# Transfers cut to multiples of sixteen rows, keys stored alone, scales ahead of the branch, and the sorted path as the fall-through

## The chip, the cores and the metric

The kernel runs on one core of a Trainium2 chip. The core has five engines with instruction streams of their own: TensorE (PE, with its weight loads shown as PEld), VectorE (DVE), ScalarE (ACT), GpSimd (POOL) and SyncE (SP), which here only issues transfers. They meet through semaphores. The metric is the device time of one execution in microseconds; times of an unchanged kernel agree within about 0.2%.

## What is computed

A chain of four residual layers over 3125 nodes with 256 features and 50,000 edges, all in float32: a graph convolution, an attention over slices, a hypergraph convolution of two steps, and a mixture of experts. The change touches the first and, by a few rows, the last. Cut to what matters here:

```python
src, dst = edges sorted by dst                      # 50,000 pairs of node numbers

x = x + gnn(layernorm(x))                           # the section of this change
    src, dst = concat(src, 0..n-1), concat(dst, 0..n-1)
    deg  = segment_sum(1, dst)
    dinv = 1 / sqrt(deg)
    agg  = segment_sum((xn @ W)[src] * dinv[src] * dinv[dst], dst)
    return relu(agg + b)
x = x + slice_attention(layernorm(x))
x = x + hypergraph_convolution(layernorm(x))
x = x + experts(layernorm(x))                       # top 2 of 8, summed into out
```

## The kernel before

**Layout.** The nodes are padded to 3200, 25 chunks (c) of 128 rows; `XR` holds x in this layout (tile `residual`), `Z` the scaled or normed rows. The last chunk has only 53 rows (`LAST`). The graph becomes a dense matrix of edge counts, source by target, built in five blocks of 640 targets (`SB`), and the aggregation is a product with it. `XH2` keeps the rows as a high and a low float16 half, so that float16 products are exact enough.

**First block.** VectorE clears the id tiles, GpSimd makes constants, and SyncE loads `dst` and `src` as 125 rows (`ER`) of 400 numbers, and the first number of each next row as 124 single numbers (`nxt`). It waits for them, and the block ends for all engines.

**Front of the main block.** VectorE and ScalarE build `triple`, three words per edge (`front_dve`, `front_act`). SyncE (`front_sp`) stores it to `packed_dram`, the keys, behind the first two groups of five row chunks, and sends the other three groups and the last 53 rows right after it. VectorE finds the start position of each group of five targets (`place`, `w_pos`). GpSimd (`front_pool`) waits for the stores (`st`) and the positions, and gathers 128 keys per group of targets in five indirect transfers into `win`. TensorE turns them (`keys_turn_pe`), VectorE compares them with node numbers (`keys_dve`), TensorE counts degrees. In between VectorE and ScalarE take row sums and squares of x, whenever a group of rows is there (`row_statistics_dve`, `row_sums_act`, `row_squares_act`). At the end VectorE writes `flag`: 1 if the edges are not sorted or a group has more than 128 of them.

**Branch.** Each engine waits for `flag`, loads it into a register and takes `If`, the general path, or `Else`, the sorted path. For these inputs it is the sorted path. The general path stands first in each instruction stream, so that the sorted one is reached by a jump.

**Sorted path.** First `scales_dve` and `scales_act`: VectorE makes `lnscale` and `lnshift`, ScalarE scales the rows of five groups (`scaled_rows_act`), VectorE cuts them into high and low halves (`low_rows_dve`: five casts L602, five subtractions L605). A quad is four groups of five targets: VectorE makes two tiles of one-hots (`quad_dve`, L498 and L499), TensorE multiplies them (`quad_pe`, L508, one of four banks), ScalarE copies the counts out (`quad_act`, L519). There are 160 quads, 32 in each block, and 16 of them (`AHEAD`) are made before the main loop. The loop runs over five blocks b and 32 slots s: each slot makes quad 16 further on and an eighth of a quarter of the aggregation (`quarter_pe`, L1111). A quarter at s = 0 or s = 16 first waits until the copies of the quads that it reads are done. Six idle products (L355) stand between the leading quads and the loop. Then follow first products, relu, residual, statistics and the normed rows for the next section.

**Last section.** Before the experts, SyncE stores the rows to `out`, 3072 rows and then the 53 (L2153); GpSimd's first accumulating scatter waits for both (`xr_st`).

## Time and profile before

| | us |
|---|---|
| median of three runs (lowest, highest) | 1334.64 (1334.37, 1336.47) |
| the profiled execution, its own time | 1334.33 |
| its span, first to last instruction | 1332.6 |
| TensorE busy (matrix products) | 1242.6, 93% |
| VectorE busy | 570.0, 43% |
| ScalarE busy | 473.7, 36% |
| GpSimd busy | 198.2, 15% |
| mean granted TensorE clock | 0.969 of full speed |

The span divides into the front and the leading quads (0 to about 68 us), the main loop of the first layer (to 264), its end (to 276), the attention (to 403), the hypergraph convolution (to 1052), the routing (to 1098) and the experts. A busy share over the whole span says little about the front, where TensorE mostly waits. In rows of the order in time, the first number is the start in us, the second the length; square brackets give the idle time of the engine before it and what ended it. PEq, DVEq and SPq are the instruction queues of these engines.

### The profile page before, as it was taken

The page shows a single profiled execution, that of the slowest core. Times are in us where ns is not written, and L with a number is a line of the kernel's source. Part 1 is how long each engine was busy: PE and PEld are TensorE (multiplying, and loading weights), DVE is VectorE, ACT ScalarE, POOL GpSimd, SP SyncE. Part 2 cuts the span into 40 slices and gives each one's busy share as a digit, 9 for nine tenths or more (in the row PEclk, how much of TensorE's full clock was granted, in tenths as well). Part 3 has the DMA queues.
Part 4 walks back from the last instruction along what each step waited for, and adds up shares of the span by engine and source line. Part 5 has one row for each costly group of instructions (what it writes and reads, how often), then busy time and mean ns, then how long its engine had stood idle before and what let it go on. Part 6 is the DMA issues. An engine that isn't in the chain of part 4 may idle for free. (4 is left out here: it accounts for less than half of the span.)

```text
span 1332.6 us, 19869 instructions
## 1 busy us (share of the span) xinstructions
PE 1242.6 (93%) x7442; PEld 844.6 (63%) x7442; DVE 570.0 (43%) x1529; ACT 473.7 (36%) x1142; POOL 198.2 (15%) x201
## 2 busy tenths in 40 slices
PE   3399999989999999999999999999999878999995
PEld 1277777745558544457777544467777547888884
DVE  5878777567764413123333333222222471222221
ACT  5765666357743787830000010001222302222221
POOL 3000000023310000000000000000000005767773
PEclk8599999999999999999999999999999889999998
DMA  5132133400003155575556445587653264666662
GB/s 178 38 124 73 56 121 125 139 28 0 1 0 126 43 157 155 154 157 126 124 128 140 128 148 149 152 188 168 143 120 68 64 198 136 146 142 149 157 156 44
DMA packets 253597, 154.91 MB, mean 116 GB/s; under 512 B 172536, under 2 KB 242375, under 8 KB 253364
## 3 DMA queue, kind: packets, MB, share of 16 engines
q1 hardware_dynamic: 242420, 138.56, 38.0%
q0 software_dynamic: 11072, 14.97, 6.1%
q8 instruction: 64, 1.05, 0.3%
q14 instruction: 41, 0.34, 0.1%
HBM read 78.48 MB, written 35.00 MB: 85 GB/s over the span
## 5 line engine op out<-in xcount | busy, mean ns | idle before, releaser
L974 PE MATMUL bank<-weights,agg_in_out 128*128 128x320 f16 x2000 | 274.8, 299 | 0.0
L988 PE MATMUL bank<-weights 128*128 128x512 f16 x1250 | 270.7, 379 | 1.2 <-issue 1.2
L974 PEld LDWEIGHTS bank<-weights,agg_in_out 128*128 128x128 f16 x2000 | 195.7, 98 | 76.2
L988 PEld LDWEIGHTS bank<-weights 128*128 128x128 f16 x1250 | 122.0, 98 | 149.3 <-DVEq L1786 1.7
L1111 PE MATMUL bank<-weights,agg_in_out 128*128 128x320 f16 x1000 | 163.2, 299 | 0.0
L804 POOL TENSOR_TENSOR shift<-shift,rstd 128x5 f32<-128x5 f32 x15 | 3.6, 243 | 914.6 <-ACT rstd L809 914.6
L519 ACT CAST weights<-bank 128x500 f16<-128x500 f32 x160 | 114.2, 723 | 68.9 <-PE bank L508 68.9
L1111 PEld LDWEIGHTS bank<-weights,agg_in_out 128*128 128x128 f16 x1000 | 91.7, 98 | 26.2
L2258 PE MATMUL bank<-weights 128*128 x448 | 105.5, 384 | 0.5 <-ACT weights L2274 0.2
L2274 ACT ACTIVATE weights<-bank,weights 128x256 f32<-128x256 f32 (+1 forms) x128 | 50.2, 444 | 155.4 <-PE bank L2243 155.4
L2243 PE MATMUL bank<-wk,weights 128*128 128x256 f32 (+1 forms) x512 | 104.2, 357 | 0.9 <-DVE wk L2289 0.9
L1784 DVE SCALAR_TENSOR_TENSOR wk<-bank,inverse_degree,wk 128x256 f32<-128x256 f32 x50 | 24.0, 480 | 181.9 <-ACT wk L1980 181.9
L2336 POOL DMA_INDIRECT out<-weights,agg_in_out x56 | 89.3, 1595 | 61.4 <-DVE weights L2304 34.5
L2243 PEld LDWEIGHTS bank<-wk,weights 128*128 128x128 f32 x512 | 89.5, 193 | 12.0 <-issue 1.2
L2258 PEld LDWEIGHTS bank<-weights 128*128 128x128 f32 x448 | 80.7, 190 | 15.9 <-issue 7.2
L1019 ACT COPY agg_in_out<-bank 128x320 f32<-128x320 f32 x20 | 8.5, 426 | 218.5 <-PE bank L974 218.5
L508 PE MATMUL bank<-wn,wk 128*128 128x125 f16 x640 | 64.8, 227 | 18.2 <-DVE wn L499 17.6
L1027 DVE COPY agg_in_out<-bank 128x320 f32<-128x320 f32 x20 | 9.8, 491 | 161.1 <-PE bank L974 141.0
L498 DVE TENSOR_TENSOR wk<-iota,low_source 128x512 f16<-128x512 f16 x160 | 67.4, 421 | 25.9 <-PE bank L508 25.1
L1980 ACT ACTIVATE wk<-bank,inverse_degree 128x256 f32<-128x256 f32 x50 | 23.6, 474 | 153.2 <-PE bank L988 142.3
L508 PEld LDWEIGHTS bank<-wn,wk 128*128 128x128 f16 x640 | 49.6, 101 | 34.3 <-DVE wn L499 22.8
L2316 POOL DMA_INDIRECT normed<-rows_and_gates,agg_in_out x56 | 59.0, 1054 | 58.5 <-POOLq L1759 41.7
(355 smaller groups left out, 1455.8 us busy)
## 6 DMA issues: line engine op xcount, KB each, us to landing
weights<-counts_source_target SPq DMA_DIRECT2D x50, 800.0 KB, 4.6
counts_source_target<-weights SPq DMA_DIRECT2D x5, 4000.0 KB, 13.9
weights<-in_L_ffn_W SPq DMA_DIRECT2D x32, 512.0 KB, 3.9
weights<-in_L_ffn_W SPq DMA_DIRECT2D x4, 1024.0 KB, 5.5
rows_and_gates<-normed SPq DMA_DIRECT2D x1, 3300.0 KB, 12.0
out<-residual SPq DMA_DIRECT2D x1, 3072.0 KB
residual<-in_x SPq DMA_DIRECT2D x4, 640.0 KB, 7.9
weights<-in_L_ffn_b SPq DMA_DIRECT2D x1, 1024.0 KB, 7.6
```

The lines of the kernel that those rows point to most:

```text
L498: nc.vector.tensor_tensor(couples(ohs[:, u]), ramp(4, P), twins(slo2[:, g, :], P), ALU.is_equal)
L508: last = nc.tensor.matmul(ps[QBANK[u]][:, t * NR:(t + 1) * NR], ohs[:, u, t, :], ohr[:, u, t, 0:NR], start=True, stop=True)
L519: nc.scalar.copy(to, ps[QBANK[q % 4]][:, 0:4 * NR].rearrange("p (t n c) -> p t c n", t=4, c=NC)).then_inc(q_ev.sem, 1)
L974: last = nc.tensor.matmul(bank, source[:, 5 * k + c, part * F + fh * P:part * F + fh * P + P], MB[:, k, c, h * HALF:(h + 1) * HALF], start ...
L988: last = nc.tensor.matmul(ps[j][:, :], MB[:, k, c, j * P:(j + 1) * P], source[:, 5 * k + c, :], start=(k == 0 and c == 0), stop=(k == 4 an ...
L1111: last = nc.tensor.matmul(bank, XH2[:, c, part * F + fh * P:part * F + fh * P + P], ats[b % 2][:, c, h * HALF:(h + 1) * HALF], start=(m == ...
L1784: step(nc.vector.scalar_tensor_tensor(t, ps[n % 5][:, 0:F], inv[:, 1, n:n + 1], wk[:, n % 2, 0:F], ALU.mult, ALU.add))
L2243: last = nc.tensor.matmul(ps[2 + 2 * b + m // 2][:, (m % 2) * w:(m % 2 + 1) * w], w1b[:, b, k, m * P:(m + 1) * P], xT[:, b, k * w:(k + 1) ...
L2258: last = nc.tensor.matmul(ps[6 + b][:, h * F:(h + 1) * F], hT[:, b, k, h * P:(h + 1) * P], w2[:, k, bass.ds(expert, 1), :].rearrange("p a ...
L2274: last = nc.scalar.activation(hT[:, b, m, 0:w], ps[2 + 2 * b + m // 2][:, (m % 2) * w:(m % 2 + 1) * w], ACT.Gelu, bias=b1T[:, bass.ds(expe ...
L2316: pool.indirect_dma_start(out=xg[:, n % 4, h, :], out_offset=None, in_=zg_dram, in_offset=bass.IndirectOffsetOnAxis(ap=row_i[:, t:t + 1], ...
L2336: pool.indirect_dma_start(out=out, in_=yb[:, n % 2, h, :], in_offset=None, out_offset=bass.IndirectOffsetOnAxis(ap=out_i[:, t:t + 1], axis=0),
```

## The change

It does seven things.

1. Transfers of 125, 124 and 53 rows are cut in two: 112 and 13, 112 and 12, 48 and 5 (`FANS`, `TAILS`). This concerns the loads of the ids, the store of the keys, the load and the store of the last rows.
2. The loads of row groups 0 and 1 move from the front of the main block to the end of the first block, behind SyncE's wait for the ids.
3. After the store of the keys SyncE waits until it has landed before it issues row groups 2 to 4.
4. The scales, and ScalarE's scaling of row group 0, move ahead of the branch.
5. ScalarE makes the high halves of row group 0 (`high_rows_act`), VectorE keeps the other four groups.
6. A second flag `fine` is the inverse of `flag`; `If` is now the sorted path, `Else` the general one, so the sorted path follows the branch and ends with a jump over the general one.
7. In block 0 each slot of the main loop does its part of the quarter ahead of its quad.

```diff
+        FANS = (slice(0, ER // 16 * 16), slice(ER // 16 * 16, ER))
+        TAILS = (slice(0, LAST // 16 * 16), slice(LAST // 16 * 16, LAST))
+
+        def rows_sp(sp, g):
+            n = 5 if g < 4 else 4
+            sp.dma_start(XR[:, 5 * g:5 * g + n, :],
+                         x[5 * g * P:(5 * g + n) * P, :].rearrange("(c p) f -> p c f", p=P)
+                         ).then_inc(x_gr[g].sem, 16)
...
-                sp.dma_start(ed[0:ER, 1, :], dst.rearrange("(p j) -> p j", j=EW)).then_inc(ld.sem, 16)
-                sp.dma_start(ed[0:ER, 0, :], src.rearrange("(p j) -> p j", j=EW)).then_inc(ld.sem, 16)
+                for k, ids_of in ((1, dst), (0, src)):
+                    for at in FANS:
+                        sp.dma_start(ed[at, k, :], ids_of.rearrange("(p j) -> p j", j=EW)[at]).then_inc(ld.sem, 16)
...
-                    sp.dma_start(nxt[0:ER - 1, :], dst[EW:E].rearrange("(p j) -> p j", j=EW)[:, 0:1]
-                                 ).then_inc(ld.sem, 16)
-                sp.wait_ge(ld.sem, 16 * 3)
-            ld.close(16 * 3)
+                    for at in (FANS[0], slice(FANS[1].start, ER - 1)):
+                        sp.dma_start(nxt[at, :], dst[EW:E].rearrange("(p j) -> p j", j=EW)[at, 0:1]
+                                     ).then_inc(ld.sem, 16)
+                sp.wait_ge(ld.sem, 16 * 6)
+                for g in range(2):
+                    rows_sp(sp, g)
+            ld.close(16 * 6)
...
+        HIGH_BY_ACT = 1
+
+        def high_rows_act(act, g):
+            act.wait_ge(z_sc.sem, 5 * g + 5)
+            for c in range(5 * g, 5 * g + 5):
+                last = nc.scalar.copy(XH2[:, c, 0:F], Z[:, c, 0:F])
+            last.then_inc(z_hi.sem, 1)
+
         def low_rows_dve(dve, step, g):
-            dve.wait_ge(z_sc.sem, 5 * g + 5)
-            for c in range(5 * g, 5 * g + 5):
-                last = nc.vector.tensor_copy(XH2[:, c, 0:F], Z[:, c, 0:F])
-            step(last)
+            if g < HIGH_BY_ACT:
+                dve.wait_ge(z_hi.sem, g + 1)
+            else:
+                dve.wait_ge(z_sc.sem, 5 * g + 5)
+                for c in range(5 * g, 5 * g + 5):
+                    last = nc.vector.tensor_copy(XH2[:, c, 0:F], Z[:, c, 0:F])
+                step(last)
             for c in range(5 * g, 5 * g + 5):
                 last = nc.vector.tensor_tensor(XH2[:, c, F:2 * F], Z[:, c, 0:F], XH2[:, c, 0:F], ALU.subtract)
             last.then_inc(a_in.sem, 1)
...
-            dve.wait_ge(d_mm.sem, 2)
-            step(nc.vector.tensor_scalar(fix[:, 0:1], ps[1][:, 65:66], float(E), None, ALU.not_equal))
-            step(nc.vector.tensor_tensor(fix[:, 0:1], fix[:, 0:1], ps[1][:, 64:65], ALU.max))
-            nc.vector.tensor_scalar(flag[:], fix[:, 0:1], 1.0, None, ALU.min).then_inc(f_out.sem, 1)
-            ch.close(step.done)
-
-        def scales_dve(dve, step):
             dve.wait_ge(l_rt.sem, 1)
             dve.wait_ge(d_rt.sem, 1)
             step(nc.vector.scalar_tensor_tensor(lnscale[:], rstd[:], FIX, dinv[:], ALU.mult, ALU.mult))
             nc.vector.tensor_tensor(lnshift[:], shift[:], lnscale[:], ALU.mult).then_inc(l_sc.sem, 1)
             nc.vector.tensor_scalar(dinvs[:], dinv[:], 1.0 / FIX, None, ALU.mult)
+
+            dve.wait_ge(d_mm.sem, 2)
+            step(nc.vector.tensor_scalar(fix[:, 0:1], ps[1][:, 65:66], float(E), None, ALU.not_equal))
+            step(nc.vector.tensor_tensor(fix[:, 0:1], fix[:, 0:1], ps[1][:, 64:65], ALU.max))
+            nc.vector.tensor_scalar(flag[:], fix[:, 0:1], 1.0, None, ALU.min)
+            nc.vector.tensor_scalar(fine[:], fix[:, 0:1], 0.0, None, ALU.is_le).then_inc(f_out.sem, 1)
+            ch.close(step.done)
+
+        def first_quads_dve(dve, step):
             dve.wait_ge(w_low.sem, NSB)
             for q in range(AHEAD):
                 quad_dve(dve, q)
...
             act.wait_ge(l_sc.sem, 1)
             scaled_rows_act(act, 0)
+            high_rows_act(act, 0)
+
+        def first_quads_act(act):
             for q in range(AHEAD):
                 quad_act(act, q)
                 if q % 3 == 2 and q < 14:
-                    scaled_rows_act(act, q // 3 + 1)
+                    g = q // 3 + 1
+                    scaled_rows_act(act, g)
+                    if g < HIGH_BY_ACT:
+                        high_rows_act(act, g)
...
-            rows(0)
-            rows(1)
             sp.wait_ge(y_ready.sem, 3)
-            sp.dma_start(packed_dram[0:E * KW].rearrange("(p j) -> p j", j=EW * KW),
-                         triple[0:ER].rearrange("p j w -> p (j w)")).then_inc(st.sem, 16)
+            for at in FANS:
+                sp.dma_start(packed_dram[0:E * KW].rearrange("(p j) -> p j", j=EW * KW)[at],
+                             triple[at].rearrange("p j w -> p (j w)")).then_inc(st.sem, 16)
+            sp.wait_ge(st.sem, 48)
             for g in range(2, 5):
-                rows(g)
-            sp.dma_start(XR[0:LAST, NC - 1, :], x[(NC - 1) * P:N, :]).then_inc(x_gr[4].sem, 16)
+                rows_sp(sp, g)
+            for at in TAILS:
+                sp.dma_start(XR[at, NC - 1, :], x[(NC - 1) * P:N, :][at]).then_inc(x_gr[4].sem, 16)
...
-            pool.wait_ge(st.sem, 32)
+            pool.wait_ge(st.sem, 48)
...
-        def branch(eng):
+        def sorted_and_sparse(eng):
             eng.wait_ge(f_out.sem, 1)
-            return general(eng)
+            return eng.value_load(fine[0:1, 0:1], min_val=0, max_val=1)
...
-                with dve.If(branch(dve)):
...
-                        normalise_dve(dve, step, l2_st, g)
-                    chg.close(step.done)
-                with dve.Else():
+                with dve.If(sorted_and_sparse(dve)):
                     step = Chain(dve, chf)
-                    scales_dve(dve, step)
+                    first_quads_dve(dve, step)
...
+                with dve.Else():
+                    step = Chain(dve, chg)
...
-                            if b == 0 and s == 0:
-                                idle_products(0, 6)
+                            if b == 0:
+                                if s == 0:
+                                    idle_products(0, 6)
+                                quarter_pe(pe, b, s // 8, s % 8)
                             if b * QB + s + AHEAD < QUADS:
                                 quad_pe(pe, b * QB + s + AHEAD)
...
-                            quarter_pe(pe, b, s // 8, s % 8)
+                            if b:
+                                quarter_pe(pe, b, s // 8, s % 8)
                             if b >= 1 and 4 <= s < 14 and s % 2 == 0:
                                 first_product_pe(pe, 5 * (b - 1) + (s - 4) // 2)
...
-                sp.dma_start(out[(NC - 1) * P:N, :], XR[0:LAST, NC - 1, :]).then_inc(xr_st.sem, 16)
+                for at in TAILS:
+                    sp.dma_start(out[(NC - 1) * P:N, :][at], XR[at, NC - 1, :]).then_inc(xr_st.sem, 16)
...
-                        pool.wait_ge(xr_st.sem, 32)
+                        pool.wait_ge(xr_st.sem, 48)
```

What stands on SyncE's queue before, from the load of single numbers to the last rows. `residual` is x, `edges_packed` the keys:

```order
L334 DMA weights<-in_dst 124x1
L266 UNCONDITIONAL_BRANCH
L1575 UNCONDITIONAL_BRANCH
L719 DMA edges_packed<-padding_keys 1x384
L715 DMA residual<-in_x 128x5x256 x2
L724 DMA edges_packed<-weights 125x1200
L715 DMA residual<-in_x 128x5x256 x2
L715 DMA residual<-in_x 128x4x256
L728 DMA residual<-in_x 53x256
```

The same stretch of SyncE's queue now:

```order
L345 DMA weights<-in_dst 112x1
L345 DMA weights<-in_dst 12x1
L272 DMA residual<-in_x 128x5x256 x2
L276 UNCONDITIONAL_BRANCH
L1604 UNCONDITIONAL_BRANCH
L744 DMA edges_packed<-padding_keys 1x384
L748 DMA edges_packed<-weights 112x1200
L748 DMA edges_packed<-weights 13x1200
L272 DMA residual<-in_x 128x5x256 x2
L272 DMA residual<-in_x 128x4x256
L754 DMA residual<-in_x 48x256
L754 DMA residual<-in_x 5x256
```

Two row loads stand now ahead of the block's end, and the key store is in two pieces; the wait behind it is not among these rows.

On VectorE's queue before, the branch stands behind the flag, and the general path follows it:

```order
L654 TENSOR_REDUCE weights<-degree 128x1
L657 TENSOR_SCALAR fix<-bank 128x1
L658 TENSOR_TENSOR fix<-fix,bank 128x1
L659 TENSOR_SCALAR flag<-fix 128x1
L768 TENSOR_LOAD flag
L768 ISA x2
L1441 COMPARE_AND_BRANCH
L396 TENSOR_SCALAR weights<-weights 128x800
```

The sorted path begins some 240 instructions further on, behind the end of the general path:

```order
L1441 UNCONDITIONAL_BRANCH
L665 SCALAR_TENSOR_TENSOR row_scale<-rstd,dinv 128x25
L666 TENSOR_TENSOR row_shift<-shift,row_scale 128x25
L667 TENSOR_SCALAR dinv_unscaled<-dinv 128x25
L498 TENSOR_TENSOR wk<-iota,low_source 128x512
```

VectorE's queue at the branch now:

```order
L679 TENSOR_REDUCE weights<-degree 128x1
L683 SCALAR_TENSOR_TENSOR row_scale<-rstd,dinv 128x25
L684 TENSOR_TENSOR row_shift<-shift,row_scale 128x25
L685 TENSOR_SCALAR dinv_unscaled<-dinv 128x25
L688 TENSOR_SCALAR fix<-bank 128x1
L689 TENSOR_TENSOR fix<-fix,bank 128x1
L690 TENSOR_SCALAR flag<-fix 128x1
L691 TENSOR_SCALAR fine<-fix 128x1
L790 TENSOR_LOAD fine
L790 ISA x2
L1467 COMPARE_AND_BRANCH
L512 TENSOR_TENSOR wk<-iota,low_source 128x512
```

The three scale operations moved ahead of the flag, and the first one-hots follow the branch directly.

TensorE's queue before, at the start of the main loop: 64 products of the leading quads, idle products, then quad and quarter in turn:

```order
L508 MATMUL bank<-wn,wk 128x125 x64
L355 MATMUL bank<-zeros,ident 128x512 x6
L508 MATMUL bank<-wn,wk 128x125 x4
L1111 MATMUL bank<-weights,agg_in_out 128x320 x6
L508 MATMUL bank<-wn,wk 128x125 x4
```

And now:

```order
L522 MATMUL bank<-wn,wk 128x125 x64
L368 MATMUL bank<-zeros,ident 128x512 x6
L1137 MATMUL bank<-weights,agg_in_out 128x320 x6
L522 MATMUL bank<-wn,wk 128x125 x4
L1137 MATMUL bank<-weights,agg_in_out 128x320 x6
```

The quarter's part (the 128x320 products) went ahead of the quad (the 128x125 products).

## Rows read from the trace of the kernel before

**Rows 1.** windows of ten us: window, length, busy us (count) by engine, PEclk, DMA share, GB/s

```profile
50.00:60.00 10.00, 3.61 (x24) 2.05 (x24) 9.93 (x35) 10.00 (x21) 0.00 (x0) 0.50 0.00 0
...
70.00:80.00 10.00, 10.00 (x102) 7.84 (x100) 7.58 (x22) 6.59 (x10) 0.00 (x0) 1.00 0.01 2
```

**Rows 2.** windows of one us, same columns

```profile
4.00:5.00 1.00, 0.00 (x0) 0.00 (x0) 0.00 (x0) 0.00 (x0) 0.84 (x6) 1.00 0.32 112
...
12.00:13.00 1.00, 1.00 (x2) 0.41 (x2) 0.96 (x3) 0.67 (x3) 0.00 (x0) 1.00 1.09 357
...
20.00:21.00 1.00, 0.00 (x0) 0.00 (x0) 0.00 (x0) 1.00 (x6) 0.00 (x0) 1.00 0.34 122
```

**Rows 3.** order in time, the keys' way through DRAM: start, length, operation

```profile
11.50 0.28 SPq L724 DMA_DIRECT2D edges_packed<-weights  x1
...
17.09 0.17 DVE L634 TENSOR_SCALAR weights<-weights 128x5 int32<-128x5 f32 x1
...
21.01 1.27 POOL L755 DMA_INDIRECT agg_in_out<-edges_packed,weights  x1 [12.82 <-DMA edges_packed<-weights]
...
26.91 0.80 PE L538 MATMUL bank<-quarter_identity,agg_in_out 128*128 128x128 f32 x2 [11.05 <-DMA agg_in_out<-edges_packed,weights]
```

**Rows 4.** order in time, end of the first block

```profile
2.60 0.34 SPq L334 DMA_DIRECT2D weights<-in_dst  x1
...
6.71 0.28 POOL L309 TENSOR_SCALAR_AFFINE_SELECT identity_shifted<-identity_shifted 64x128 f32<-64x128 f32 x1
...
7.78 0.98 SPq L715 DMA_DIRECT2D residual<-in_x  x2
```

**Rows 5.** the gathers' line L755: queue instruction, and landing of its transfers

```profile
L755 POOLq MOVE  x5: 29/29/29, 20.1 to 22.4; - x5
...
DMA to landing us min/median/max: 3.1/3.7/5.9
```

**Rows 6.** tile residual to 50 us, landing of its loads

```profile
DMA to landing us min/median/max: 4.5/7.9/11.2
```

**Rows 7.** DMA issues: name, count, KB each, median us to landing

```profile
weights<-in_L_ffn_W SPq DMA_DIRECT2D x32, 512.0 KB, 3.9
...
weights<-in_L_ffn_W_q SPq DMA_DIRECT2D x2, 16.0 KB, 2.0
```

**Rows 8.** order in time, flag and first one-hots

```profile
38.62 0.15 DVE L659 TENSOR_SCALAR flag<-fix 128x1 int32<-128x1 f32 x1
40.40 0.19 DVE L665 SCALAR_TENSOR_TENSOR row_scale<-rstd,dinv 128x25 f32<-128x25 f32 x1 [1.62 <-issue]
...
40.84 2.56 ACT L596 ACTIVATE normed<-residual,row_shift,row_scale 128x256 f32<-128x256 f32 x5 [3.06 <-DVE row_shift L666]
42.71 0.18 DVE L667 TENSOR_SCALAR dinv_unscaled<-dinv 128x25 f32<-128x25 f32 x1 [1.91 <-issue]
42.80 0.42 DVE L498 TENSOR_TENSOR wk<-iota,low_source 128x512 f16<-128x512 f16 x1
```

**Rows 9.** line L1541, TensorE's branch: ns min/median/max, start

```profile
L1541 PEldq COMPARE_BRANCH  x1: 4189/4189/4189, 39.7 to 39.7; - x1
```

**Rows 10.** order in time: casts on VectorE, the same form on ScalarE, quad 16

```profile
46.80 1.10 DVE L602 CAST agg_in_out<-normed 128x256 f16<-128x256 f32 x5
...
68.34 0.60 PE L508 MATMUL bank<-wn,wk 128*128 128x125 f16 x4 [0.32 <-DVE wn L499]
...
445.13 1.63 ACT L1988 ACTIVATE weights<-normed 128x256 f16<-128x256 f32 x5
```

**Rows 11.** order in time, a quad and its copy in the main loop

```profile
70.66 0.38 PE L508 MATMUL bank<-wn,wk 128*128 128x125 f16 x4
...
71.08 0.73 ACT L519 CAST weights<-bank 128x500 f16<-128x500 f32 x1 [0.31 <-PE bank L508]
```

**Rows 12.** order in time, TensorE's first products of the attention

```profile
276.44 3.17 PE L1250 MATMUL bank<-weights,tT 128*128 128x512 f32 x4 [3.51 <-ACT tT L1209]
...
280.50 1.98 PE L1250 MATMUL bank<-weights,tT 128*128 128x512 f32 x4 [0.46 <-ACT tT L1209]
```

105 lines of the change are left out of this document (51 added, 54 removed).

## Prediction

> **What bounds the kernel now.** I read the windows first, since all edits but one lie in the first 70 us and in the stretch behind them, then the order in time, and last the queues' own instructions. From about 68 to 264 us TensorE is the bound: 10.00 us busy in every ten, at full clock [rows 1]. Work saved on another engine there is worth nothing, and whatever makes TensorE wait there costs its full length. Before 68 us TensorE is at half clock and waits, and the path runs elsewhere: the edge numbers arrive; keys of three words are built, stored to DRAM at 11.50 and gathered again by GpSimd from 21.01; TensorE turns the first gathered block at 26.91 [rows 3]; VectorE compares keys; then come degrees, flag and branch. The sixteen leading quads are paced by VectorE, 9.93 us busy in ten where TensorE has 3.61 [rows 1]. What is won or lost by the end of this section passes to the end of the kernel at its full size, since each later section starts where the one before it ends.
>
> **The change, part by part.** The sum is made against the profiled execution: 1334.33 us, its span 1332.6 us.
>
> *First block, 0.* Six loads replace three. Loads of 125 rows keep a share of 0.32 of the sixteen DMA engines, that is five of them; transfers of 128 rows fill all [rows 2]. Six issues of 0.34 us from 1.8 on end near 4.0 [rows 4]; at the 2.0 us that a small load takes [rows 7] the last is in at 6.0; the two row loads now issued in this block take 0.98 us, to 7.0. GpSimd's constants end at 6.99 [rows 4], so the block ends when it did, 0.2 us either way.
>
> *Key store, 2.8.* GpSimd's registers for the gathers are set at 20.1 [rows 5], so the store had landed by then; the first gather begins 0.9 us later [rows 3]. The store runs on five engines among row loads. With 112 and 13 rows and nothing behind it, it should behave as the 512 KB loads, 3.9 us [rows 7], scaled to 586 KB 4.5 us, and with a second issue of 0.3 us it lands at 16.3. Then the other thing that the gathers wait for is late: the positions, at 17.09 + 0.17 = 17.26 [rows 3]. With the same 0.9 us the gathers start at 18.2 instead of 21.0: 2.8 us. Bounds: 0, if a store to DRAM goes at that pace on any number of engines, and 2.8; I take 2.8, since the share of 0.32 counts engines.
>
> *First gather's landing, 0.5.* It takes 5.9 us today, the median is 3.7 [rows 5]; five engines still drain row loads beside it (0.34 at 20 us [rows 2]). Afterwards row groups 2 to 4, 1.8 MB, are issued behind the store, at about 16.3, and move until about 22 at the 357 GB/s of [rows 2], again beside the gathers. Between 3.7 (a gain of 2.2) and the row loads' own median of 7.9 [rows 6] (a loss of 2.0) I take 5.4, close to today's own row: 23.6. VectorE's statistics of row group 2 must be done by then: issued at 16.3, landed by 20.8 (the quickest row load took 4.5 [rows 6]), 2.5 us of work, 23.3. Free, but narrowly. ScalarE's row sums start earlier than today and end in front of the keys.
>
> *Scales ahead of the branch, and the branch, 2.7.* The flag is ready at 38.77, the first operation of the sorted path starts at 40.40, and after two short operations VectorE stands for 1.91 us with "issue", waiting for nothing that the profile shows; the one-hots start at 42.80 [rows 8]. Ahead of the branch the three scale operations run while VectorE would wait for TensorE's 128x2 product; with `fine` the flag comes some 0.15 us later. Without a jump the one-hots should start after load and compare alone, about 1.2 us behind the flag: 38.77 + 0.15 + 1.2 = 40.1, which is 2.7 us. Bounds: 0.8 if the 1.91 us stay, 2.7 if they go. They stand two operations behind a jump over the general path and nowhere else in these 70 us, so I take 2.7. TensorE's own jump lasted 4.19 us, from 39.7 to 43.9 [rows 9], and would hold the first quad even if VectorE were early; it no longer jumps here.
>
> The Trainium skill ("Runtime: NRT & Kernel Launch", section Instruction fetch mechanics) says that instructions stream in sequence, and that a taken branch to outside the two loaded pages must fetch its target first. By that rule the 1.91 us go, as in the sum, but the sorted path now has to jump over the general one at its end, and the stall comes back there. The same skill ("Advanced Engine Details and Errata", section Control Flow Timing) gives a compare-and-branch about 108 ns; by that figure alone this term would be near 0, and the row of 4.19 us speaks against it.
>
> *ScalarE makes the first high halves, 1.1.* VectorE loses five casts, 1.10 us [rows 10], of a stretch in which it is the bound. ScalarE scales group 0 (2.56 us [rows 8]) from about 38.3 to 40.9, before the branch, and adds five casts, 1.63 us by the same form [rows 10], to 42.6; its own branch is hidden behind them. It then starts its quad copies 2.5 us behind VectorE's first one-hots and has four scalings and sixteen copies of 0.73 [rows 11] ahead, 21.9 us, where VectorE has some 23.7 (42.80 to about 67.6, less 1.1); it is early at each later meeting but the first. If it is late there, that costs up to 0.6.
>
> *Quarter ahead of quad at the start, 0.3.* TensorE ends its six idle products and waits 0.32 us for quad 16 [rows 10]. Now it has a quarter's part to do meanwhile.
>
> *Quarter ahead of quad later, -1.3.* Two new waits. At s = 16 of block 0 the quarter's part needs 32 copies, and quad 31 is now multiplied directly before it. A copy starts 0.04 us behind its quad (70.66 + 0.38 to 71.08) and takes 0.73 [rows 11]: with the semaphore about 0.85 us, where today a quarter's part and the next quad lie between. At s = 0 of block 1 the old order is back; quad 48 (0.38 us) stands between quad 47 and the part that needs its copy: 0.45 us. TensorE is the bound, so both count in full, and what queues behind its wait, the next quads, has four banks of slack. Bounds: -0.4, if TensorE has slack that its modelled ends hide, and two whole copies with semaphores, -1.8.
>
> *Jump at the end of the sorted path, 0.* TensorE's jump, 4.19 us by [rows 9], comes behind its last products; the idle products that end at 272.9 today (276.44 - 3.51 [rows 12]) move by up to that, to 277.1 at the latest, about where ScalarE's first copy of tokens lets TensorE go on. Today it idles 3.51 us before that point, and its first four products take 3.17 us instead of 1.98 [rows 12]; the pause only moves ahead. If the clock then stays up, 1.2 us are won; if it falls while the idle products run, some 0.6 are lost. ScalarE's jump falls behind five queued normalisations of 2.56 us in all: a stall of 1.91 is hidden, one of 4.19 costs 1.9. I take 0.
>
> *Last rows' store, 0.* One more issue on SyncE behind 3 MB of stores; the next section starts long after SyncE is through.
>
> Sum: 2.8 + 0.5 + 2.7 + 1.1 + 0.3 - 1.3 = 6.1 us. 1334.33 - 6.1 = 1328.2; the median of the three runs lies 0.3 above the profiled one: **1328.5 us**.
>
> **The rivals.**
> *The stall moves with the code.* The 1.91 us come back behind the branch, or ScalarE's 1.9 us at the closing jump lie on the path. For it: TensorE's jump of 4.19 us. Against: ScalarE took the same branch and began its scalings as soon as row_shift was there [rows 8]. Gain 4.2: 1330.4.
> *The store does not get faster.* The gathers start as today and the first two terms fall away: gain 2.8, 1331.8. For it: no row shows a small store's own pace. The Trainium skill ("DMA: Bandwidth & Descriptors", Rules for kernel authors) says of two transfers to disjoint partition halves: "Don't bother", they serialize. By that rule the split brings nothing, which is this rival. The share of 0.32 at 125 rows speaks against it.
> *Slower: the new order in block 0 costs in each slot.* If TensorE, between quarter and quad, waited in each of the 32 slots for the 0.31 us that ScalarE waits before a copy [rows 11], block 0 would lose 9.9 us: 1334.6 - 6.1 + 9.9 = 1338.4. It decides from 0.19 us a slot. Against it: quarter, quad, quarter is the same ring as before, and a quad waits only for the copy of four quads earlier.
> *More than forecast.* The clock stays up at 276 (1.2) and the first gather lands in 3.9 us (1.5): gain 8.8, 1325.8.
>
> **How the numbers follow.** Forecast 0.64; stall moves 0.14; store no faster 0.07; more 0.09; several at once, a net within 2.7 us of before, 0.03; slower 0.03. The range 1325.6 to 1331.4 holds the forecast with its unknown gather and jump, the first rival and most of the fourth. About 0.2% (2.7 us) is what a measurement of this kernel can tell from no change: faster 0.92, same 0.05, slower 0.03.
>
> **What would show it.** GpSimd's first gather near 18.2 and TensorE's first turn near 23.6; no TensorE compare of 4 us at the branch; one-hots 1.3 us behind the flag and no gap of 1.91 us; the main loop's first quarter near 61; one wait of 0.85 us and one of 0.45 us for ScalarE's copies; a TensorE jump of about 4 us behind the last products near 263. Wrong would be a first turn later than 25, or a main loop longer by more than 2 us.

## The result, and the profile after

The changed kernel takes 1328.16 us (median of five runs, 1327.97 to 1328.91), the kernel before 1336.31 us in the runs beside it (1334.37 to 1336.62). The ratio is 0.9946, 95% interval 0.9935 to 0.9957: faster by 5.7 to 8.7 us. The prediction said 1328.5, range 1325.6 to 1331.4. The two profiled executions are 1334.33 and 1328.36 us, 5.97 apart. Their spans, 1332.6 and 1326.6, are 6.0 apart, and it is these two traces that the sum of 6.1 spoke of.

The head of the page after: span, then busy time of each engine.

```profile
span 1326.6 us, 19878 instructions
...
PE 1244.7 (94%) x7442; PEld 845.3 (64%) x7442; DVE 568.6 (43%) x1525; ACT 475.1 (36%) x1147; POOL 198.2 (15%) x201
```

The order in time of the front (start, length, operation), the lines that answer to [rows 3, 8, 10]:

```profile
11.30 0.77 SPq L748 DMA_DIRECT2D edges_packed<-weights  x2
...
14.83 1.53 SPq L272 DMA_DIRECT2D residual<-in_x  x3
...
18.18 1.27 POOL L781 DMA_INDIRECT agg_in_out<-edges_packed,weights  x1 [10.19 <-DVE weights L659]
...
23.79 0.80 PE L552 MATMUL bank<-quarter_identity,agg_in_out 128*128 128x128 f32 x2 [7.72 <-DMA agg_in_out<-edges_packed,weights]
...
35.54 0.15 DVE L690 TENSOR_SCALAR flag<-fix 128x1 int32<-128x1 f32 x1
35.61 0.14 DVE L691 TENSOR_SCALAR fine<-fix 128x1 int32<-128x1 f32 x1
36.81 0.43 DVE L512 TENSOR_TENSOR wk<-iota,low_source 128x512 f16<-128x512 f16 x1 [1.06 <-issue]
...
57.75 0.60 PE L522 MATMUL bank<-wn,wk 128*128 128x125 f16 x4 [2.88 <-DVE wn L513]
58.14 2.77 PE L368 MATMUL bank<-zeros,ident 128*128 128x512 f16 x6
...
60.70 1.81 PE L1137 MATMUL bank<-weights,agg_in_out 128*128 128x320 f16 x6
```

Each row is a step. SyncE issues the remaining row groups at 14.83, when the keys have landed, 3.5 us behind their store. The gathers start at 18.18 instead of 21.01 and now wait for the positions (L659) instead of the store. The one-hots start 1.20 us behind `fine`, 1.27 behind `flag` (at 35.54), where the one-hots stood 4.18 behind `flag` [rows 8]. The last leading quad is at 57.75, and the loop's first part of a quarter at 60.70. Then the loop and what follows it, TensorE alone:

```profile
80.41 0.97 PE L1137 MATMUL bank<-weights,agg_in_out 128*128 128x320 f16 x6 [0.90 <-ACT weights L533]
...
99.14 0.97 PE L1137 MATMUL bank<-weights,agg_in_out 128*128 128x320 f16 x6 [0.68 <-ACT weights L533]
...
258.27 0.30 PE L1137 MATMUL bank<-weights,agg_in_out 128*128 128x320 f16 x1
...
267.34 0.57 PE L1253 MATMUL bank<-ident,normed 128*128 128x128 f32 x2 [2.67 <-issue]
...
272.32 1.88 PE L1276 MATMUL bank<-weights,tT 128*128 128x512 f32 x4
...
274.88 1.98 PE L1276 MATMUL bank<-weights,tT 128*128 128x512 f32 x4 [0.46 <-ACT tT L1235]
```

The first two are the new waits for ScalarE's copies. In the trace before the loop has none, and its last product is at 263.29. The pause of 2.67 us is the closing jump. The two last rows answer to [rows 12]: 272.32 for 276.44, 274.88 for 280.50.

What each trace shows at seven points, in us. "Loop" is the first product behind the idle products, "last product" the start of the loop's last one:

| kernel | first gather | first turn | last flag operation | first one-hots | quad 15 | loop | last product |
|---|---|---|---|---|---|---|---|
| before | 21.01 | 26.91 | 38.62 | 42.80 | 64.86 | 68.34 | 263.29 |
| changed | 18.18 | 23.79 | 35.61 | 36.81 | 57.75 | 60.70 | 258.27 |
| cuts_only | 18.05 | 23.06 | 34.76 | 39.62 | 61.68 | 65.16 | 259.86 |
| uncut_alone | 20.75 | 27.20 | 40.72 | 41.92 | 62.85 | 65.80 | 263.50 |
| cut_120 | 18.05 | 24.34 | 36.16 | 37.36 | 58.28 | 61.23 | 258.17 |
| no_store_wait | 18.70 | 22.25 | 34.08 | 35.28 | 56.21 | 59.16 | 256.38 |
| general_first | 18.07 | 23.84 | 35.65 | 39.72 | 60.65 | 63.60 | 260.98 |
| high0 | 18.06 | 23.91 | 35.73 | 36.93 | 59.00 | 61.96 | 259.86 |
| high2 | 18.05 | 24.06 | 35.88 | 37.07 | 58.23 | 61.19 | 257.78 |
| old_order | 18.04 | 23.80 | 35.61 | 36.81 | 57.73 | 61.21 | 255.91 |
| order_to_8 | 18.65 | 23.84 | 35.66 | 36.86 | 57.79 | 60.74 | 256.88 |
| order_to_8_idle2 | 18.12 | 24.27 | 36.10 | 37.30 | 58.23 | 59.64 | 256.80 |
| no_wait_old_order | 18.05 | 22.49 | 34.31 | 35.51 | 56.45 | 59.92 | 255.45 |
| no_wait_order8_warm | 18.28 | 22.74 | 34.56 | 35.76 | 56.69 | 58.22 | 254.06 |

And the times, each against runs of the kernel before on the same chip:

| kernel | median us | before, median us | ratio, 95% interval |
|---|---|---|---|
| cuts_only | 1332.60 | 1335.04 | 0.9980 (0.9971 to 0.9988) |
| uncut_alone | 1333.00 | 1335.04 | 0.9986 (0.9977 to 0.9994) |
| general_first | 1332.41 | 1335.04 | 0.9984 (0.9974 to 0.9994) |
| old_order | 1328.41 | 1335.04 | 0.9952 (0.9940 to 0.9965) |
| no_store_wait | 1327.40 | 1335.93 | 0.9937 (0.9925 to 0.9950) |
| order_to_8 | 1326.34 | 1335.93 | 0.9924 (0.9911 to 0.9937) |
| order_to_8_idle2 | 1326.10 | 1335.93 | 0.9924 (0.9912 to 0.9937) |
| cut_120 | 1328.74 | 1335.93 | 0.9950 (0.9937 to 0.9963) |
| high0 | 1328.40 | 1335.50 | 0.9947 (0.9934 to 0.9960) |
| high2 | 1327.82 | 1335.50 | 0.9941 (0.9928 to 0.9954) |
| no_wait_old_order | 1326.10 | 1335.50 | 0.9930 (0.9917 to 0.9943) |
| no_wait_order8_warm | 1323.23 | 1335.50 | 0.9911 (0.9899 to 0.9924) |

Executions of one kernel lie up to 6.6 us apart (old_order 1325.45 to 1329.22, general_first 1329.72 to 1336.33); one of high2's six, 1676.19 us at a mean granted clock of 0.742, is left out of its row. My reading of the spread stands at the end. An effect of one microsecond can't be read from these medians. It is read from the first table, between two points of one trace, and the medians say only whether it disagrees.

### The profile page after: what moved, and what is told of

Read it like the earlier page. It is cut to its first block and busy times, and to the rows that moved or that the text cites. A ratio compares the mean times of both kernels' runs of the same rounds, so it can differ in the third digit from the quotient of the medians.

```text
span 1326.6 us, 19878 instructions
## 1 busy us (share of the span) xinstructions
PE 1244.7 (94%) x7442; PEld 845.3 (64%) x7442; DVE 568.6 (43%) x1525; ACT 475.1 (36%) x1147; POOL 198.2 (15%) x201
## 3 DMA queue, kind: packets, MB, share of 16 engines
q8 instruction: 64, 1.05, 0.3%
```

## The experiments

### The transfers: the cut, being alone, and the wait

**cuts_only**: the kernel before, with the cuts and nothing else.

```diff
+            for at in FANS:
+                sp.dma_start(packed_dram[0:E * KW].rearrange("(p j) -> p j", j=EW * KW)[at],
+                             triple[at].rearrange("p j w -> p (j w)")).then_inc(st.sem, 16)
             for g in range(2, 5):
                 rows(g)
```

> The kernel before with the cuts into multiples of sixteen rows alone (ids, key store, last rows), everything else where it was: the store still shares the DMA engines with row groups 0 to 4. Theory A (a transfer of 125 rows keeps five of the sixteen engines busy, one of 112 all of them): the store lands about 2 us earlier than before even among the row loads, the first gather starts near 19.2 instead of 21.0 and the time is 1.5 to 2 us below before. Theory B (the width doesn't matter, the store is late because row loads share the engines with it): the gather starts at 21.0 and the time is that of before within 0.3 us.

Measured: the gathers start at 18.05 and the time is 0.2% below before, median 2.4 us. Theory A, and more than it asked for. The store lands in time even between row loads (before, it was the last to come, [rows 3]):

```profile
18.05 1.27 POOL L761 DMA_INDIRECT agg_in_out<-edges_packed,weights  x1 [10.06 <-DVE weights L638]
...
23.06 0.80 PE L542 MATMUL bank<-quarter_identity,agg_in_out 128*128 128x128 f32 x2 [7.76 <-DMA agg_in_out<-edges_packed,weights]
```

The gather waits for the positions here too, and the first turn comes 0.73 us *earlier* than in the changed kernel, where the store is alone.

**uncut_alone**: the changed kernel, with whole transfers.

```diff
-        FANS = (slice(0, ER // 16 * 16), slice(ER // 16 * 16, ER))
-        TAILS = (slice(0, LAST // 16 * 16), slice(LAST // 16 * 16, LAST))
+        FANS = (slice(0, ER),)
+        TAILS = (slice(0, LAST),)
```

> The changed kernel with whole transfers again (125, 124 and 53 rows), but still with row groups 0 and 1 ahead, the store alone and the wait behind it. Theory A: the store of 586 KB at the 120 GB/s that five engines move takes about 5 us plus some 2 of start, so it lands at 18 to 18.5, later than the positions at 17.2; the first gather starts near 19, row groups 2 to 4 start 3.5 us later than in the changed kernel, and the time is 0.8 to 1.5 us above it. Theory B: the store lands at about 15 as in the changed kernel, the gather starts at 18.2, the time is that of the changed kernel.

Measured: theory A in its kind, but larger. The gathers start at 20.75, later than A said, and nearly all that the cut gave is gone; the median is 4.8 us above the changed kernel's, where A said 0.8 to 1.5. SyncE's store and the row groups behind its wait, and the gather:

```profile
12.95 0.27 SPq L748 DMA_DIRECT2D edges_packed<-weights  x1
19.85 2.62 SPq L272 DMA_DIRECT2D residual<-in_x  x3
20.75 1.27 POOL L781 DMA_INDIRECT agg_in_out<-edges_packed,weights  x1 [11.13 <-DMA edges_packed<-weights]
```

Two things add up. The ids land later too, and the row loads behind them end the first block later, so VectorE's first cast starts at 8.98 instead of 7.34; and the store takes 6.9 us from issue to landing, 12.95 to 19.85, instead of 3.5. Then row group 2 is issued 5.0 us later than in the changed kernel, and VectorE takes its statistics at 24.62, ahead of the first keys: from the first turn to the flag it is 13.5 us instead of 11.8. Alone and whole, the store makes the last flag operation 2.1 us later than before. The median is 2 us below before all the same, though the loop ends 0.2 later; more than the 0.95 us that the changed kernel gains behind its loop, and I can't place the rest.

**cut_120**: 120 and 5 rows instead of 112 and 13.

```diff
-        FANS = (slice(0, ER // 16 * 16), slice(ER // 16 * 16, ER))
+        FANS = (slice(0, 120), slice(120, ER))
```

> The changed kernel with ids and keys cut in 120 and 5 rows instead of 112 and 13. Theory A (a transfer spreads over as many engines as divide its rows: five for 125, sixteen for 112): 120 rows have eight or fifteen of sixteen engines, a share of 0.5 to 0.94 while the store moves, and it lands at 15.0 to 16.5, the positions at 17.2 still being last; the last quarter ends within 0.8 of 258.27. Theory B (any cut into two transfers does it): the store lands at 14.8 as in the changed kernel, at a share of 1. Theory C (only multiples of sixteen rows are spread): it lands at 18 or later and the gathers start after 19.

Windows of one microsecond while the store moves: window, length, busy us (count) of PE, PEld, DVE, ACT, POOL, clock, DMA share, GB/s. In order: the changed kernel, cut_120, uncut_alone.

```profile
12.00:13.00 1.00, 1.00 (x3) 0.47 (x2) 0.97 (x3) 0.97 (x7) 0.00 (x0) 1.00 0.96 278
```

```profile
12.00:13.00 1.00, 1.00 (x3) 0.47 (x2) 0.96 (x3) 0.97 (x7) 0.00 (x0) 1.00 0.92 202
```

```profile
15.00:16.00 1.00, 1.00 (x3) 0.49 (x2) 0.93 (x4) 1.00 (x5) 0.00 (x0) 1.00 0.33 120
```

112 rows hold a share of 0.96, 120 rows 0.92, 125 rows 0.33. The traces' DMA packets say it more plainly. The store is 125 packets of 4800 bytes, and for most of its time sixteen of them are in flight at once in the changed kernel, fifteen in cut_120, and five in uncut_alone and in the kernel before. With 120 and 5 the wait behind the store ends at 15.32, where the seven traces with 112 and 13 and this wait have 14.80 to 14.90: theory A, and theories B and C fall. It is not the multiple of sixteen that matters but how many engines a row count spreads over. That the last product, at 258.17, is as early as in the changed kernel is luck: the one-hots are 0.55 later, and the clock, as the loops' table below shows, gives about 0.6 back. The Trainium skill ("DMA: Bandwidth & Descriptors", section Why a DMA increments its semaphore by 16 and not by 1) says that a transfer uses the largest number of engines up to sixteen that divides the slowest dimension of both its sides: sixteen for 112 rows, fifteen for 120, five for 125. By that rule the shares would be, as an estimate, 1.00, 0.94 and 0.31, and the packets in flight agree with it, the three rows within 0.04. "Don't bother", the rule that the prediction weighed, does not hold for this cut, which changes the number of engines.

**no_store_wait**: the changed kernel without SyncE's wait.

```diff
-            sp.wait_ge(st.sem, 48)
             for g in range(2, 5):
```

> The changed kernel without SyncE's wait for the stored keys: row groups 2 to 4 and the last rows are issued right behind the store, cut in two as it is. Theory A (from the run with the cuts alone, whose first turn came at 23.06 against 23.79: the wait only pushes the row loads onto the gathers): the gathers still start near 18.1, the positions being last, the first turn comes near 23.1, the flag 0.8 earlier, the last quarter ends 0.7 earlier than the changed kernel's 258.27. Theory B (the store needs the engines to itself): the gathers start 0.5 to 1.5 us later and the last quarter ends later than 258.3.

```profile
12.18 2.41 SPq L272 DMA_DIRECT2D residual<-in_x  x3
...
18.70 1.27 POOL L780 DMA_INDIRECT agg_in_out<-edges_packed,weights  x1 [10.66 <-DVE weights L659]
...
22.25 0.80 PE L552 MATMUL bank<-quarter_identity,agg_in_out 128*128 128x128 f32 x2 [5.58 <-DMA agg_in_out<-edges_packed,weights]
```

The gather starts 0.5 us later than in the changed kernel, which looks like theory B, but it waits for the positions and not for the store, and the start says nothing of the wait: it is 18.05, 18.28 and 18.70 in the three kernels without the wait, and 18.04 to 18.65 in those with it and the cut in 112. Its keys land in 3.55 us instead of 5.61 (in the other two without the wait, 4.44 and 4.46), so the first turn comes 1.5 us earlier: theory A, at twice its size. In the three kernels without the wait the last flag operation is at 34.08, 34.31 and 34.56, in the seven that have it and the cut in 112 at 35.61 to 36.10. Between the medians, 34.31 and 35.66, the wait costs 1.35 us: it moves the row loads from beside the store, which need not hurry, to beside the gathers, which must. The median is 0.8 us below that of the changed kernel, whose runs stand beside others; that alone decides nothing.

### The branch and the scales

**general_first**: the changed kernel with the general path ahead of the sorted one in the instruction streams; the scales stay ahead of the branch. On every engine:

```diff
-                with dve.If(sorted_and_sparse(dve)):
-                    step = Chain(dve, chf)
-                    first_quads_dve(dve, step)
+                with dve.If(general_flag(dve)):
+                    step = Chain(dve, chg)
...
+                with dve.Else():
+                    step = Chain(dve, chf)
+                    first_quads_dve(dve, step)
```

> The changed kernel with the general path first in the instruction streams again, so that the sorted path is reached by a jump and does not jump at its end; scales stay ahead of the branch. Theory A (the 1.91 us behind the branch and TensorE's 4.19 us compare belong to the jump): a stall of about 1.9 us returns two operations behind VectorE's branch, TensorE's compare lasts 4 us again, the end of the leading quads is 2 to 3 us later; the pause of 2.7 us ahead of the attention's first turn goes, the clock falls there again (0.6 us); time 1330.5 to 1331.5. Theory B (the stall belonged to the scale operations): one-hots start 0.6 us later than in the changed kernel, nothing else, 1328.8.

VectorE's first one-hots, and TensorE's branch (durations in ns):

```profile
39.72 0.42 DVE L512 TENSOR_TENSOR wk<-iota,low_source 128x512 f16<-128x512 f16 x1 [3.93 <-issue]
```

```profile
L1567 PEldq COMPARE_BRANCH  x1: 4209/4209/4209, 36.7 to 36.7; - x1
```

TensorE's two compares in the changed kernel, at the branch and at the closing jump:

```profile
L1567 PEldq COMPARE_BRANCH  x2: 78/1907/3736, 36.7 to 263.5; - x2
```

Theory A in its size, not in its place. The stall stands now in one piece directly behind the branch, 3.93 us with the flag operations done, against 1.06 in the changed kernel. So the fall-through is worth 2.9 us. From the end of the flag to the one-hots it is 4.03 us before and 3.93 here: against this trace, moving the three scale operations ahead of the jump gains 0.1 us. They had lain inside the stall. But the stall itself is not the same each time. In cuts_only, where branch and scales are as before, the two gaps are 1.62 and 2.59 us, TensorE's compare is 4.83, and from flag to one-hots it is 4.71:

```profile
39.53 0.18 DVE L671 TENSOR_SCALAR dinv_unscaled<-dinv 128x25 f32<-128x25 f32 x1 [2.59 <-issue]
```

Against that trace the scales would gain 0.8. So their share is 0.1 to 0.8 us, and more than these traces can tell apart; that the jump has the larger part holds either way. The median, 1332.41, is 1 to 2 us above what A said.

**high0 and high2**: the high halves of no group (the diff), or of two, on ScalarE.

```diff
-        HIGH_BY_ACT = 1
+        HIGH_BY_ACT = 0
```

> The changed kernel with all five groups of high halves on VectorE again. Theory A (five casts of 0.22 us on the engine that bounds the leading quads): from the first one-hots to the last leading quad 1.1 us longer than the changed kernel's 20.94, i.e. 22.0, and the last quarter ends 1.1 later. Theory B (the branch hid them, or ScalarE is the bound): no difference.

From the first one-hots to quad 15 it is 22.07 us instead of 20.94: 1.13 for five casts, theory A. The last product is 1.59 later, of which 0.34 is the clock at the loop's start (below). The median, 1328.40, does not show it.

> The changed kernel with the high halves of two groups on ScalarE. Theory A (VectorE stays the bound; ScalarE has some 22 us of work against VectorE's 21): first one-hots to last leading quad 0.3 to 1.1 us shorter than 20.94. Theory B (ScalarE becomes the bound, since its copies then come after VectorE's one-hots): 0.3 to 1.6 longer.

21.16 us, 0.22 *longer* than with one group. VectorE's only waits in this stretch besides the branch:

```profile
45.57 1.77 DVE L630 TENSOR_TENSOR agg_in_out<-normed,agg_in_out 128x256 f16<-128x256 f32 x5 [0.72 <-ACT agg_in_out L618]
...
49.79 1.10 DVE L627 CAST agg_in_out<-normed 128x256 f16<-128x256 f32 x5 [0.46 <-ACT normed L610]
```

1.18 us of new waits for ScalarE take back what five fewer casts give. For the leading quads one group is the right number; the medians of the three kernels, 1328.40, 1328.16 and 1327.82, don't tell them apart.

### The order of quad and quarter

**old_order**: quad ahead of quarter in all slots. **order_to_8**: quarter ahead of quad in the first eight slots only (the diff; old_order has `s < 0`).

```diff
+                            ahead = b == 0 and s < 8
-                                quarter_pe(pe, b, s // 8, s % 8)
+                            if ahead:
+                                quarter_pe(pe, b, s // 8, s % 8)
...
-                            if b:
+                            if not ahead:
                                 quarter_pe(pe, b, s // 8, s % 8)
```

> The changed kernel with quad ahead of quarter in block 0 again. Theory A (each of the two waits costs 1.05 us for good, the start of the loop gains nothing that the clock does not take back): loop starts with quad 16 at 61.2, no wait for copies at s = 16 and at block 1, end of the last quarter about 2 us earlier, time near 1326.2. Theory B (the rows' idle of 0.90 and 0.68 is made up elsewhere, and the start is worth 0.5 us): the time is 1328.2 to 1328.7.

> The changed kernel with quarter ahead of quad in the first eight slots of block 0 only. Theory A (the two waits behind two quads in a row cost 1.05 us each and the order costs nothing else): no wait for copies at s = 16 and at block 1, start of the loop at 60.7 as in the changed kernel, end of the last quarter at 256.2. Theory B (the old order's 2.36 us came from the start, where the first parts ran at half clock): end of the last quarter at 258.3 less at most 0.5.

old_order's last product is at 255.91, 2.36 us earlier than in the changed kernel, from a loop that starts 0.51 later: its profile says theory A. Its median is 1328.41 and says nothing of it, so the gain is shown for the loop and not for the whole time. (Of the 2.36, 1.00 is the clock, as follows.) order_to_8 has no wait either, yet ends at 256.88, between the two expectations. The clock makes the difference. Windows around the loop's start, same columns as above: old_order, the changed kernel, order_to_8.

```profile
60.00:61.00 1.00, 0.86 (x3) 0.00 (x0) 1.00 (x4) 0.00 (x0) 0.00 (x0) 0.65 0.00 0
```

```profile
62.00:63.00 1.00, 1.00 (x9) 0.77 (x8) 1.00 (x4) 0.08 (x1) 0.00 (x0) 0.65 0.00 0
```

```profile
63.00:64.00 1.00, 1.00 (x6) 0.65 (x5) 0.88 (x3) 0.72 (x1) 0.00 (x0) 0.66 0.00 0
```

0.65 in a window means that the clock stood at its lower level, 1.2 GHz, for the first 0.70 us of it and at 2.4 behind. So it was up at 60.70, 62.70 and 63.68, in code that is the same up to the loop. What of the loop runs at half clock costs half its length. With 194.70 us for a loop at full clock (old_order) and one number for the two waits, 1.89 (from the changed kernel: 197.57 - 194.70 - half of 2.00 = 1.87; from no_store_wait: 197.22 - 194.70 - half of 1.26 = 1.89), the loops come out; of the rows below, only the changed kernel's went into these numbers:

| kernel | clock full from | loop at half clock | two waits | worked out | measured |
|---|---|---|---|---|---|
| before | 68.88 | 0.54 | no | 194.97 | 194.95 |
| cuts_only | 64.56 | 0 | no | 194.70 | 194.70 |
| order_to_8 | 63.68 | 2.94 | no | 196.17 | 196.14 |
| no_wait_old_order | 61.66 | 1.74 | no | 195.57 | 195.53 |
| changed | 62.70 | 2.00 | yes | 197.59 | 197.57 |
| uncut_alone | 68.06 | 2.26 | yes | 197.72 | 197.70 |
| general_first | 65.20 | 1.60 | yes | 197.39 | 197.38 |
| cut_120 | 61.94 | 0.71 | yes | 196.95 | 196.94 |
| high0 | 64.64 | 2.68 | yes | 197.93 | 197.90 |
| high2 | 61.18 | 0 | yes | 196.59 | 196.59 |

The waits and the clock account for the whole length; the order costs nothing else in its 32 slots. The two kernels that are not in the table wait for the one-hots of quad 16 as well. With that wait order_to_8_idle2 comes to 197.13 (4.58 us up to the clock's rise, 0.29 of them a wait) and measured 197.16, no_wait_order8_warm to 195.68 (a wait of 0.98 at full clock) and measured 195.84.

**order_to_8_idle2**: the same with two idle products instead of six.

```diff
-                                    idle_products(0, 6)
+                                idle_products(0, 2)
```

> As the run before it, with two idle products ahead of the loop instead of six. In the changed kernel VectorE's one-hots of quad 16 are ready at 61.17, and the six idle products hold the first quarter's part until 60.7 although its rows are ready. Theory A: the first part starts 1.8 us earlier at half clock, TensorE then waits for quad 16 until 61.2, and the rest follows about 1.1 us earlier: end of the last quarter at 255.1. Theory B (the idle products are what lifts the clock): it rises later than 62.3, and the gain is lost, 256.2 or more.

Theory B in its number. The first part starts earlier, at 59.64, 1.41 us behind quad 15 instead of 2.95, but the clock is up only at 64.22, and the last product is at 256.80 against 256.88. Its cause isn't shown: the clock is up 5.99 us behind quad 15 here, and 2.88 to 5.89 in the twelve kernels with six idle products there and none before, so one trace can't say that four fewer products delayed it.

**no_wait_old_order**: no wait behind the store, and the old order.

> The changed kernel without the wait for the stored keys and with quad ahead of quarter throughout. If the two effects are independent (1.5 us in front of the leading quads; two waits of 1.05 us in the loop), the loop starts at 59.7 to 60.2, lasts 194.7 us plus half of what it runs at half clock, and the last quarter starts its last product at 254.2 to 255.0; time 1325.0 to 1326.0, below the changed kernel. If they are not, it stays above 255.9, the value with the order alone.

The front is 1.3 us earlier and the loop has no wait: the two effects add up. The last product is at 255.45, 0.45 later than expected, since 1.74 us of the loop ran at half clock.

**no_wait_order8_warm**: no wait behind the store, quarter ahead in eight slots, and idle products in TensorE's last two pauses among the leading quads.

```diff
                     for q in range(AHEAD):
                         quad_pe(pe, q)
+                        if q in (11, 14):
+                            idle_products(0, 6)
```

> Without the wait for the stored keys, quarter ahead of quad in the first eight slots, and six idle products more behind each of the leading quads 11 and 14, in pauses of TensorE of 2.9 us. Theory A (what TensorE did in the microseconds before sets when the clock rises): it rises before the loop starts, the loop starts near 59.2 and lasts 194.7 us, its last product starts at 253.9. Theory B (the rise comes by chance or by time alone): the clock is still at half for the first 1 to 3 us of the loop, 254.5 to 255.4.

The clock's rise, then TensorE in time:

```profile
52.00:53.00 1.00, 0.88 (x8) 0.45 (x7) 1.00 (x4) 1.00 (x3) 0.00 (x0) 0.73 0.00 0
```

```profile
56.69 0.39 PE L522 MATMUL bank<-wn,wk 128*128 128x125 f16 x4 [1.79 <-DVE wn L513]
...
58.22 0.98 PE L1136 MATMUL bank<-weights,agg_in_out 128*128 128x320 f16 x6
...
60.17 0.39 PE L522 MATMUL bank<-wn,wk 128*128 128x125 f16 x4 [0.98 <-DVE wn L513]
...
254.06 0.30 PE L1136 MATMUL bank<-weights,agg_in_out 128*128 128x320 f16 x1
```

Theory A for the clock. It is up at 52.54, over five microseconds ahead of the loop and 4.15 ahead of quad 15, outside all that the other traces show, and stays up through the loop. The six idle products behind quad 15 then end sooner, and the loop starts at 58.22, with one wait of 0.98 us for the one-hots of quad 16. The loop starts 1.0 us earlier than expected and lasts 195.84 instead of 194.7; the last product is at 254.06 where 253.9 was expected. The kernel takes 1323.23 us, ratio to before 0.9911 (0.9899 to 0.9924), and all its runs (1322.00 to 1324.43) are below all of the changed kernel's: it beats both. Their mean granted clock is 0.975 or 0.976 in all five, in those of no_wait_old_order 0.970 or 0.971, so the early rise is not one trace's luck. What the idle products alone are worth was not run: without them and with the old order it is 1326.10.

## Why the prediction was right, point by point

The number was right, 1328.5 for 1328.16, and 6.1 us for 5.97 between the traces, in part by luck: the loop lost 1.3 us more than the sum had, and 0.95 us behind the loop, which the sum put at nothing, made most of it good. The sign of being wrong that the prediction named for this came, too: a main loop longer by more than 2 us. It is 2.62 longer.

| step | predicted us | measured us |
|---|---|---|
| first gather earlier | 2.8 | 2.83 |
| first gather's landing | 0.5 | 0.29 |
| first turn to flag | 0 | -0.04 |
| flag to one-hots | 2.7 | 2.91 |
| one-hots to quad 15 | 1.1 | 1.12 |
| loop starts earlier behind quad 15 | 0.3 | 0.53 |
| two waits in the loop | -1.3 | -1.89 |
| loop at half clock | not in the sum | -0.73 |
| behind the loop | 0 | 0.95 |
| sum | 6.1 | 5.97 |

- **First block, key store.** 18.18 for 18.2, bounded by the positions as said. The share of 0.32 as five engines was the right reading. The store was quicker than the row loads that I scaled from: landed at 14.8, not 16.3. What I did not see is that the cut alone does it. I argued "112 and 13 rows *and nothing behind it*", and the second half of that buys nothing.
- **The gather's landing.** 5.61 us for 5.4. I put this term as a gain, since today's row was 5.9. In truth SyncE's wait is what keeps it there: without it the landing takes 3.55, 4.44 and 4.46 in three traces. The bound of 3.7 was in the text, but as something that the change might reach, not as something that one of its edits prevents.
- **Scales and branch.** Size right, share wrong. I gave the term to both edits; general_first shows the jump at 2.9 us and the scales at 0.1, or at 0.8 if cuts_only stands for before. I read the two gaps of 1.62 and 1.91 us [rows 8] as a fixed load and compare and one stall. They were one stall, cut in two by two short operations. The Trainium skill's rule on taken branches ("Runtime: NRT & Kernel Launch", section Instruction fetch mechanics), that a target outside the loaded pages must be fetched first, agrees with it: 3.93 us with the jump, 1.06 without. Whether VectorE's target, some 240 instructions further on, lay outside them no trace shows. TensorE's compare went from 4.19 us to 78 ns.
- **High halves.** 1.12 and 1.13 for 1.1.
- **The order of quad and quarter, the step that failed.** Both waits are where I put them. The gain over before shrinks by 1.05 us across s = 16 (7.13 to 6.08 at the identity products, now L1134, of the slots 15 and 23). Across the start of block 1 it shrinks by 1.05 more, of which 0.22 is the place of one quad (from 70.66 [rows 11] to the next product at 70.88), so 0.83; together the 1.89 of the loops' lengths. I had said 0.85 and 0.45. For the second I let quad 48 hide half of ScalarE's copy; it does not, since the two quads run back to back in 0.60 us. And the rows' own idle time, 0.90 and 0.68, is below the cost, since matmul ends are modelled.
- **The clock at the loop's start** had no term. 2.00 us of the loop run at half clock, where it was 0.54: 0.73 us lost. Starting 0.53 closer to quad 15 explains at most 0.27 of that. The rest is that the clock rose 4.95 us behind quad 15 instead of 4.02, and over the twelve kernels with the same products up to there it rose 2.88 to 5.89 behind it. So the order costs 1.89 in its waits and gives 0.53 at the start, less up to 0.27: a loss of 1.4 to 1.6 us where I had forecast one of 1.0. The other 0.5 us is the clock's later rise, which the order doesn't explain.
- **The closing jump.** As said, it lies beside ScalarE's way. The gain is 5.02 us at the loop's last product and at ScalarE's first normalisation, L356 (268.55 for 273.57), with TensorE's compare at 3.74 us in between. What the prediction named as a possible 1.2, the clock staying up at the attention's first products, came as 0.6: those four took 1.88 instead of 3.17 us but were held by idle products that ran at half clock (4.78 us for 3.19). In general_first, without that jump, the clock was down there for twice as long.

The error in the order was made good by 0.95 us behind the loop, of which 0.6 is this clock and the rest is spread: 5.7 us at the end of the attention, 5.9 at the end of the hypergraph convolution, 6.0 at the end. The rest I can't place.

The rivals: the store was faster; the stall did go; the order costs at two points and not in each slot, as the table of the loops shows. Of the two parts of "more than forecast", the clock gave half and the landing in 3.9 us did not come.

## What to carry to other kernels

Look at the row count of a transfer that others wait for, and at the DMA share while it runs: 125 rows held a third of the engines, 112 and 13 nearly all. Here a transfer that is on the path wanted its competitors *before* the next one on the path, not behind a wait that pushed them onto it. Before moving operations ahead of a branch, ask whether they already lie in its stall; and where an engine is to start a long stretch at full clock, give it idle products in the pauses just ahead, not only at the last moment.

## What the runs showed of the hardware

- **The width of a transfer** follows its row count: shares of 0.96, 0.92 and 0.33 and sixteen, fifteen and five packets in flight for 112, 120 and 125 rows, and the store of 586 KB took 3.5, 4.0 and 6.9 us.
- **A jump over the general path.** From flag to one-hots VectorE took 3.93, 4.03 and 4.71 us in the three traces that have the jump there, and 1.06 in the changed kernel; TensorE's compare took 4.2 to 4.8 us, and 0.08 without. The closing jump, 3.3 to 3.8 us on TensorE in all traces that have it, took nothing from the gain at ScalarE's first normalisation in the changed kernel.
- **The clock's rise is not at a fixed distance.** In the twelve kernels whose TensorE makes the same products up to the loop, it rose 2.88 to 5.89 us behind quad 15, and the loop ran at half clock for 0 to 2.9 us. And it falls in some traces at places where it stays up in others: behind the first loop it fell in twelve of the fourteen traces, but not in no_wait_old_order and no_wait_order8_warm, and in the attention's last products in three, cuts_only, high2 and no_wait_old_order. In cuts_only it fell in the attention's last products:

```profile
394.00:396.00 2.00, 1.92 (x10) 0.96 (x10) 1.12 (x4) 0.33 (x1) 0.00 (x0) 0.91 0.00 0
396.00:398.00 2.00, 2.00 (x7) 0.84 (x5) 0.42 (x1) 0.37 (x1) 0.00 (x0) 0.50 0.00 0
398.00:400.00 2.00, 2.00 (x8) 1.72 (x7) 0.00 (x0) 0.00 (x0) 0.00 (x0) 0.73 0.00 0
```

  At shares of 0.91, 0.50 and 0.73 that is 1.7 us of full clock lost; the trace before has 1.00 in this section's end:

```profile
398.00:400.00 2.00, 1.92 (x12) 1.00 (x10) 0.87 (x3) 0.37 (x1) 0.00 (x0) 1.00 0.00 0
```

  From the loop's last product to the end of the attention it is 141.7 us in cuts_only and 139.9 in the trace before, 1.8 longer. Such a fall, present or not, is as large as most terms of this case, and is my reading of why executions of one kernel differ by several us; no run here tests it alone. The Trainium skill ("TensorE: Matmul & The Clock Gate", section What's actually happening) says that one kernel shows other numbers of slow products from run to run, and the traces agree.
